# First adjacency sweep: the column sums' two halves added on VectorE, one degree matmul a tile

## What is computed

```python
A_hat = adj + jnp.eye(adj.shape[0], dtype=adj.dtype)
d_inv_sqrt = jnp.sum(A_hat, axis=1) ** (-0.5)
A_norm = d_inv_sqrt[:, None] * A_hat * d_inv_sqrt[None, :]
support = x @ W.T
out = A_norm @ support
return jax.nn.relu(out)
```

## Time and profile before

| | |
|---|---|
| median of 3 runs | 1946.84 us (1945.93 to 1947.46) |
| the profiled execution, its own time | 1950.9 us |
| its span, first to last instruction | 1949.1 us |
| mean granted TensorE clock | 0.965 |
| first sweep, in the span | to about 221 us |
| busy in the whole span | PE 1807.9, DVE 1616.5, ACT 1331.3, POOL 959.1 us |

### The profile page before, as it was taken

One profiled execution on the slowest core, in us unless ns is written; L12 is line 12 of the kernel. 1 busy time (PEld: TensorE's weight loads), 2 busy tenths in 40 slices (PEclk: granted clock), 3 DMA queues, 4 the chain that ended last, 5 costly groups with the idle time before them and its releaser, 6 DMA issues. The chain is left out here.

```text
span 1949.1 us, 41788 instructions
## 1 busy us (share of the span) xinstructions
PE 1807.9 (93%) x12680; PEld 1702.0 (87%) x12680; DVE 1616.5 (83%) x4226; ACT 1331.3 (68%) x2651; POOL 959.1 (49%) x1703
## 2 busy tenths in 40 slices
PE   6799999829999999858999979999999999999997
PEld 4689999829999999857888869999999999999997
DVE  5689878739999999738656559999999999999996
ACT  4434555416666666543555459999999999999995
POOL 2000134535555555530101027777777777777774
PEclk8889999959999999979999999999999999999999
DMA  8676778237887887543556400000000000000002
GB/s 310 207 250 201 218 200 179 96 136 215 233 234 232 236 237 228 133 170 104 193 173 203 143 17 2 2 2 2 2 1 2 2 2 2 2 2 2 2 2 71
DMA packets 97235, 226.26 MB, mean 116 GB/s; under 512 B 20897, under 2 KB 51363, under 8 KB 88620
## 3 DMA queue, kind: packets, MB, share of 16 engines
q1 hardware_dynamic: 82476, 206.33, 33.8%
q0 software_dynamic: 14592, 17.91, 4.7%
HBM read 204.43 MB, written 19.75 MB: 115 GB/s over the span
## 5 line engine op out<-in xcount | busy, mean ns | idle before, releaser
L2028 PE MATMUL ffn_psH<-ffn_w2h,ffn_vTh 128*128 128x256 f32 x1320 | 393.0, 298 | 1.5 <-DVE ffn_u L2084 1.5
L2028 PE MATMUL ffn_psH<-ffn_w2h,ffn_vTl 128*128 128x256 f32 x1320 | 374.3, 284 | 0.0
L2028 PE MATMUL ffn_psH<-ffn_w2l,ffn_vTh 128*128 128x256 f32 x1320 | 373.9, 283 | 0.0
L2117 POOL TENSOR_SCALAR ffn_vn<-ffn_vn,ffn_rstd,ffn_shift 128x256 f32<-128x256 f32 x540 | 300.0, 560 | 21.1 <-issue 1.2
L2072 DVE BATCH_NORM_STATS2 ffn_stats<-ffn_vn 128x6 f32<-128x256 f32 x780 | 284.5, 406 | 25.0 <-ACT ffn_vn L2054 23.9
L2084 DVE SCALAR_TENSOR_TENSOR ffn_u<-ffn_th,ffn_psH 128x512 f32<-128x512 f32 x390 | 263.5, 676 | 7.4 <-ACT ffn_th L2051 7.4
L2028 PEld LDWEIGHTS ffn_psH<-ffn_w2h,ffn_vTh 128*128 128x128 f32 x1320 | 253.0, 192 | 2.5 <-DVE ffn_u L2084 1.7
L2028 PEld LDWEIGHTS ffn_psH<-ffn_w2l,ffn_vTh 128*128 128x128 f32 x1320 | 253.2, 192 | 0.8
L2028 PEld LDWEIGHTS ffn_psH<-ffn_w2h,ffn_vTl 128*128 128x128 f32 x1320 | 252.5, 191 | 0.0
L2054 ACT ACTIVATE ffn_vn<-ffn_u 128x512 f32<-128x512 f32 x390 | 248.7, 638 | 0.8 <-DVE ffn_u L2084 0.8
L2051 ACT ACTIVATE ffn_th<-ffn_psH 128x512 f32<-128x512 f32 x390 | 232.6, 596 | 1.7 <-PE ffn_psH L1991 1.7
(11 more groups left out here) (240 smaller groups left out, 5021.6 us busy)
## 6 DMA issues: line engine op xcount, KB each, us to landing
g_raw<-in_adjt SPq DMA_DIRECT2D x168, 384.0 KB, 4.8
g_raw<-in_wide SPq DMA_DIRECT2D x78, 512.0 KB, 3.7
moe_w1raw<-in_wall SPq DMA_DIRECT2D x33, 1024.0 KB, 5.2
moe_w2raw<-in_wall SPq DMA_DIRECT2D x33, 1024.0 KB, 5.9
moe_b<-in_eb SPq DMA_DIRECT2D x33, 128.0 KB, 4.5
g_raw<-in_adjl SPq DMA_DIRECT2D x14, 256.0 KB, 2.8
g_raw<-in_narrow SPq DMA_DIRECT2D x13, 256.0 KB, 2.6
xn_rows<-rt_hn SPq DMA_DIRECT2D x8, 384.0 KB, 4.2
```

The costliest lines, as they stand in the source:

```text
L2028: last = pe.matmul(psH[w % R][:, q * D:(q + 1) * D], a[:, w % R, q * KD + k, :], b[:, k, :], start=(k == 0 and j == 0), stop=(k == KD - 1 ...
L2117: last = pool.tensor_scalar(vn[:, t, :], vn[:, t, :], rstd[:, s:s + 1], shift[:, s:s + 1], ALU.mult, ALU.add)
```

## The change

ScalarE's `column_sum` now copies only the second half of a panel's sums (128x384) to SBUF. A new VectorE step `fold` waits for that copy and adds the first half to it, out of PSUM, into the same buffer. TensorE's `degrees` waits for the fold and runs one matmul a tile in place of two. The steps stand later: the fold at place 2 of the next panel, TensorE's degrees at place 3 in place of 2, VectorE's at 5 in place of 4; in the second sweep the fold at turn 1, TensorE's degrees at turn 2, VectorE's at 4, the scaling at 7. Waits that protected the sums' PSUM space now wait for the fold.

```diff
--- before.py
+++ after.py
@@ -193,7 +193,7 @@
         lo = sb("g0_lo", [P, SPLITS, PANEL], F32R)
         out_t = sb("g0_out_t", [P, KD, PANEL])
         delta = sb("g0_delta", [P, PT, D])
-        colsum = sb("g0_colsum", [P, CT, PANEL])
+        colsum = sb("g0_colsum", [P, PANEL])
         rowsum = sb("g0_rowsum", [1, PANEL])
         w = sb("g0_w", [P, KD, D])
         xn = sb("g0_xn", [P, 2, D])
@@ -253,7 +253,7 @@
         rstd0_done, shift0_done, norm0_done = sem("rstd0"), sem("shift0"), sem("norm0")
         xn_done, xtr_done, xnT_done, xmm_done, sup_done = (sem(n) for n in ("xn", "xtr", "xnT", "xmm", "sup"))
         dve_added, pe_added = sem("dve_added"), sem("pe_added")
-        colsum_done, deg_mm, deg_added, deg_done = sem("colsum"), sem("deg_mm"), sem("deg_added"), sem("deg")
+        colsum_done, folded, deg_mm, deg_added, deg_done = (sem(n) for n in ("colsum", "folded", "deg_mm", "deg_added", "deg"))
         dinv_done, root_done = sem("dinv"), sem("root")
         sh_done, sl_done = sem("sh"), sem("sl")
         diag_done, hi_done, lo_done, mm_done = sem("diag"), sem("hi"), sem("lo"), sem("mm")
@@ -456,7 +456,7 @@
                 act.wait_ge(dve_added, dve_sum_of(q, dve_places(q)[-1]))
                 if q >= 1:
                     act.wait_ge(deg_mm, q)
-                last = act.activation(colsum[:, :, 0:v], deg_acc[q % 2][:, :, 0:v], ACT.Copy)
+                last = act.activation(colsum[:, 0:v], deg_acc[q % 2][:, 1, 0:v], ACT.Copy)
                 if PE_SUMS[q]:
                     act.wait_ge(pe_added, sum(PE_SUMS[:q + 1]))
                     last = act.activation(rowsum[:, 0:v], psP[0:1, 0:v], ACT.Copy)
@@ -579,11 +579,16 @@
                 dve.wait_ge(loaded[n % RING], n // RING * 16 + 16)
                 if at == 1:
                     if q >= 2:
-                        dve.wait_ge(colsum_done, q - 1)
+                        dve.wait_ge(folded, q - 1)
                     dve.tensor_tensor(to, chunk(dve_places(q)[0]), chunk(i), ALU.add).then_inc(dve_added, 1)
                 elif at > 1:
                     dve.wait_ge(dve_added, dve_sum_of(q, i) - 1)
                     dve.tensor_tensor(to, to, chunk(i), ALU.add).then_inc(dve_added, 1)
+
+            def fold(q):
+                v = width(q)
+                dve.wait_ge(colsum_done, q + 1)
+                dve.tensor_tensor(colsum[:, 0:v], deg_acc[q % 2][:, 0, 0:v], colsum[:, 0:v], ALU.add).then_inc(folded, 1)
 
             def degrees(q):
                 tiles = span_of(q)
@@ -764,7 +769,9 @@
                     for a, j in enumerate(early(q, i)):
                         split_low(early_before(q, i) + a, item(q, i), j % CT, width(q))
                     if q >= 1:
-                        if i == 4:
+                        if i == 2:
+                            fold(q - 1)
+                        if i == 5:
                             degrees(q - 1)
                         if i == 7:
                             scale_s(q - 1)
@@ -780,9 +787,11 @@
                     add_identity(m + 8)
                 if m < TURNS:
                     split_low(EARLY + m, ITEM2[m], row_tile(m) % CT, width(ORDER[PLACE[m]]))
-                if m == 3:
+                if m == 1:
+                    fold(GROUPS - 1)
+                if m == 4:
                     degrees(GROUPS - 1)
-                if m == 6:
+                if m == 7:
                     scale_s(GROUPS - 1)
                 if m == 12:
                     dve.wait_ge(root_done, 1)
@@ -902,11 +911,10 @@
                 last.then_inc(xmm_done, 1)
 
             def degrees(q):
-                pe.wait_ge(colsum_done, q + 1)
+                pe.wait_ge(folded, q + 1)
                 for i, t in enumerate(tiles_of(q)):
-                    for a in range(CT):
-                        last = pe.matmul(psD[:, t:t + 1], colsum[:, a, i * P:(i + 1) * P], g.ones[:, 0:1], start=(a == 0),
-                                         stop=(a == CT - 1 and not PE_SUMS[q]))
+                    last = pe.matmul(psD[:, t:t + 1], colsum[:, i * P:(i + 1) * P], g.ones[:, 0:1], start=True,
+                                     stop=not PE_SUMS[q])
                     if PE_SUMS[q]:
                         last = pe.matmul(psD[:, t:t + 1], rowsum[0:1, i * P:(i + 1) * P], g.ones[0:1, 0:1], start=False,
                                          stop=True)
@@ -975,7 +983,7 @@
 
             for q in range(GROUPS):
                 for i in range(CHUNKS):
-                    if i == 2 and q >= 1:
+                    if i == 3 and q >= 1:
                         degrees(q - 1)
                     if i in pe_places(q):
                         add_chunk(q, i)
@@ -993,7 +1001,7 @@
                         if 1 <= t <= NT:
                             support(t - 1)
             for m in range(END):
-                if m == 1:
+                if m == 2:
                     degrees(GROUPS - 1)
                 if m < TURNS:
                     k, j = PLACE[m], row_tile(m)
@@ -1001,7 +1009,7 @@
                         if k == 0:
                             pe.wait_ge(part_done, GROUPS - 1)
                         elif k == 1:
-                            pe.wait_ge(colsum_done, GROUPS)
+                            pe.wait_ge(folded, GROUPS)
                         else:
                             pe.wait_ge(evicted, k - 1)
                     if k == 0 and j % PT == 0:
```

## The result

| | before | changed |
|---|---|---|
| median | 1946.93 us (1943.36 to 1949.59, 10 runs) | 1942.61 us (1940.10 to 1943.76, 10 runs) |
| profiled execution, own time / span | 1950.9 / 1949.1 us | 1942.8 / 1941.0 us |

The ratio is 0.9976, with a 95% interval of 0.9969 to 0.9984: faster by 3.1 to 6.0 us. The forecast was 1943.4, or -3.4 us.

A forecast was written before the change was run, and what follows sets the result against it. No single engine bounds the sweep; TensorE or VectorE leads panel by panel. Terms -1.2 - 0.8 + 0 + 0.5 - 1.4 - 0.5 = -3.4 us take the 1946.84 median to 1943.4 us, range 1940.8 to 1947.4.

The forecast's parts named there:

- the rival that had the clock give more: Panel 3's half-clock stretch ends, say, 3.4 us sooner, freeing 1.7 us of work: -5.1 us, 1941.7; chance 0.15.
- Panel 1: First sweep, panel 1: six fewer TensorE passes save 0.70 us, the wait for ScalarE's copy is covered: -0.7 us.
- Panel 2: Panel 2 to panel 3's start: the late loads move by the same -0.7 us, hiding anything else panel 2 gains or loses.
- Panels 3 and 4: Sum reaches -1.2 us after panel 3, TensorE the bound; panel 4's degrees end 0.8 us sooner, making -2.0.
- I take -1.2, near the second: Panel 3: -2.1 us if the half-clock stretch moves with the work, -1.05 if it ends near 102; -1.2 taken.
- Panel 5: Panel 5: the degree wait of 0.43 us is about the fold's price and VectorE does not idle behind it: 0.
- Panel 6: Panel 6: VectorE is full with no degree wait to give back, TensorE's six passes become idle time: +0.5 us.
- Panels 7, 8 and the last degrees: Panels 7 and 8: TensorE leads, twice -0.7 us; second sweep's last degrees: four passes fewer, -0.5 us.
- The moved places: Degrees one place later: same price in panel 1, about 1 us later for VectorE in panel 3 but slack; no term.
- VectorE becomes the bound in panels 7 and 8: Those panels each cost a fold instead of saving 0.7 us, last degrees give nothing: about -0.5 us, 1946.3; chance 0.23.
- VectorE ends every panel: From panel 3 on, degrees behind twelve matmuls, no wait given back, every fold paid: slower, 1950.9 us; chance 0.10.
- signs of being wrong: Panel 4's degree wait unshortened; TensorE idle for low parts in panels 3, 7 or 8; half-clock stretches other than 88 to 102.

The follow-up runs named there:

- places_kept: Changed kernel with TensorE's and VectorE's degrees back at their old places and the fold at place 1: 1940.36 us, ratio 0.9963 against the kernel before.
- fold_one: Kernel before with half copy, fold and single matmul a tile only for panel 2's sums: 1945.0 us, ratio 0.9988.
- moves_only: Kernel before with the degrees one place later as in the change, but no fold: 1947.42 us, ratio 1.0007.
- passes4: Changed kernel with three more matmuls a tile against a zero column, 208 passes for 52: 1961.74 us, ratio 1.0077 against the kernel before.
- fold2: Changed kernel with one more unread 128x384 VectorE add ahead of each fold: 1944.44 us, ratio 0.9991 against the kernel before.
- experiment 9: Changed kernel with the slot table's 73-row filling issued as two transfers, 64 and 9 rows: 1939.3 us, ratio 0.9961 against the kernel before.

## Why the prediction was right, and where it was not

The sum forecast -3.4 us; the medians show -4.3, the stages -5.1. The measured time lies in the forecast's own range, 1942.0 to 1944.3, but that is in part luck: panels 3 and 4 gave 2.1 us more than their terms, panels 5 to 8 with the last degrees 0.6 less, and -5.1 is the sum of the rival that had the clock give more.

**Panel 1: right.** Forecast -0.7, measured -0.74 (16.78 to 16.04). The changed kernel's TensorE timeline shows the step with the degrees, against the earlier trace rows:

```profile
50.94 1.10 PE L910 MATMUL g_psR<-g_w,g_xnT 128*128 128x256 f32 x4 [0.35 <-ACT l_s L452]
51.87 0.72 PE L916 MATMUL g_psT<-ones,g_colsum 128*128 128x1 f32 x6
52.71 1.03 PE L910 MATMUL g_psR<-g_w,g_xnT 128*128 128x256 f32 x4
```

It lasts 52.71 - 50.94 = 1.77 us; 1.75 was forecast. The new wait of 8.66 us for ScalarE's copy cost nothing that shows in this stage, as argued. The Trainium skill, page "TensorE: Matmul & The Clock Gate", section "Back-to-back issue gap", gives its 81 ns for a matmul of 128 columns, while the passes here have one. The 0.74 us for six passes, 0.12 each, decides for the row.

**Panel 2: right.** To panel 3's first add it gives 0.2 beyond panel 1's 0.7: the landing moved along with the train ahead of it.

**Panels 3 and 4: the failed step.** Beyond their starts, the forecast had about -0.5 for panel 3 and -0.8 for panel 4; measured are -1.3 and -2.0. The step was "I take -1.2, near the second, because the stretch begins at 88, before TensorE's first matmul of the panel". It asked only where the half-clock stretch stands, at fixed length, and put a shorter one among the rivals, with a stretch ending 3.4 us sooner. It was 10 us shorter (13.7 to 3.4). With it the bound changed: the forecast had TensorE without a gap in panel 3, and VectorE's lateness as slack. In the changed kernel VectorE waits for nothing behind the panel's first add, and TensorE stands for its low part:

```profile
98.34 0.45 PE L939 MATMUL g_acc<-g_hi,g_sh 128*128 128x384 f32 x1 [1.52 <-DVE g_lo L616]
```

Shown is that the stretch at panel 3's start is short in every execution with the folds everywhere, and long in every one of before. It is also shown that its length doesn't depend on the degrees' place alone: places_kept has it short with before's place. Nor does the number of narrow passes in panel 3 order it. That is 18 in before (12 of line 908, 6 of line 911) and 12 in the changed kernel, but fold_one has 12 too and kept 10.2 us, moves_only has 18 and showed 6.8 and 3.4, and passes4 has 30 and showed 3.4 twice. One rival fits all eleven profiles with the late load and was not tested: the moment at which the clock falls. In the three of before it fell 0.6 to 1.2 us ahead of TensorE's first matmul of the panel, in moves_only 1.2 and in fold_one 0.6; there the stretch lasted 6.8 us or longer. In places_kept, fold2 and passes4 it fell 0.2 to 0.35 ahead, in the three of the changed kernel with that matmul or up to 0.45 behind it; there it lasted 3.4. Whether the change sets this moment, and whether the moment sets the length, stays open. What the 10 us are worth can't be separated cleanly either. The two panels gave 3.4 us where the forecast, at before's clock, had 1.3; the 2.1 left over are what the clock and the shifted order account for together.

**Panel 5: near, by luck.** Forecast 0, measured -0.3. Two of the three executions of before have two half-clock stretches of 3.4 us in or next to this panel; the third has none and took 22.88. Against that one, with the clock alike, the changed kernel's 23.2 is 0.3 *longer*.

**Panel 6: the number right.** Forecast +0.5, measured +0.7. TensorE was busy 20.53 of 22.00 us and now

```profile
145.90:168.50 22.60, 19.77 (x113) 18.81 (x112) 22.08 (x41) 10.69 (x22) 0.85 (x1) 1.00 0.73 229
```

so its idle time went from 1.5 to 2.8, the forecast's "some 1 us"; VectorE stays full. But the +0.5 holds for the place at which the change puts the fold, not for the fold as such: places_kept takes 21.93 us here, before 21.89. In both kernels the first low part starts 2.2 us after the panel's first add (2.15 in before), and with the old places the fold stands ahead of it, in time that VectorE loses there anyway (VectorE's timeline of places_kept):

```profile
143.90 0.96 DVE L583 TENSOR_TENSOR g_psT<-g_raw 128x768 f32<-128x768 f32 x1
144.77 0.55 DVE L591 TENSOR_TENSOR g_colsum<-g_acc,g_colsum 128x384 f32<-128x384 f32 x1
...
146.10 1.02 DVE L616 TENSOR_TENSOR g_lo<-g_raw,g_hi 128x384 fp32r<-128x384 f32 x2
```

In the changed kernel, whose panel 6 starts at 145.94, it stands behind the low parts and costs 149.53 - 149.06 = 0.47 us:

```profile
148.11 1.03 DVE L616 TENSOR_TENSOR g_lo<-g_raw,g_hi 128x384 fp32r<-128x384 f32 x2
149.06 0.55 DVE L591 TENSOR_TENSOR g_colsum<-g_acc,g_colsum 128x384 f32<-128x384 f32 x1
149.53 0.96 DVE L586 TENSOR_TENSOR g_psT<-g_psT,g_raw 128x768 f32<-128x768 f32 x1
```

**Panels 7, 8 and the last degrees: too much.** Forecast were -0.7, -0.7 and -0.5, that is -1.9; measured is -1.25. The step that failed is that moving the places is free ("TensorE leads; VectorE's wait of 1.43 pays for its fold"). With the old places it does come to -1.8 (57.29 against 59.05), and moved places without the fold lose 0.7. So the terms fit the fold, and the move takes a part back.

**The moved places** were costed at nothing, and take 2.9 us by the table of places_kept. TensorE stands for low parts within panels 5 and 6 of the changed kernel:

```profile
138.67 0.45 PE L939 MATMUL g_acc<-g_hi,g_sh 128*128 128x384 f32 x1 [2.25 <-DVE g_lo L616]
...
160.77 0.44 PE L939 MATMUL g_acc<-g_hi,g_sh 128*128 128x384 f32 x1 [1.69 <-DVE g_lo L616]
```

places_kept has shorter ones at both places:

```profile
136.62 0.44 PE L939 MATMUL g_acc<-g_hi,g_sh 128*128 128x384 f32 x1 [1.38 <-DVE g_lo L616]
...
158.08 0.44 PE L939 MATMUL g_acc<-g_hi,g_sh 128*128 128x384 f32 x1 [1.07 <-DVE g_lo L616]
```

In panel 6 it is mostly the fold's place (above). In the other panels, which of the moved pieces does it (the fold, TensorE's degrees or VectorE's) was not tried apart.

**The rivals.** "The clock gives more" came in part, as a larger term inside the forecast's course, and was given back in the moved places. "VectorE becomes the bound in panels 7 and 8" did not come: no wait stands before the degrees at 177.06, and the stage shrank. "VectorE ends every panel" did not come either; but its mechanism, degrees behind twelve matmuls and low parts late, is what panels 3, 5 and 6 show in small, and all that is left of the change once the late load is gone (experiment 9). The degree wait in panel 4 fell from 2.81 to 1.01 us, just over the limit of 1 us that I had set. Two of the signs of being wrong did show: TensorE stood 1.52 us for a low part in panel 3, and the half-clock stretch was another than at 88 to 102.

## What to carry to other kernels

When two engines share the lead, price an edit per stage, and price the reordering that comes with it as an edit of its own: here, by the stage lengths, the kernel with the fold at the old places was about 8 us shorter in the sweep, some of it by the clock, and the new places that came with the change cost 2.9. A stretch at half clock in the profile of before is not fixed: state it as a range of lengths, and profile both kernels several times before crediting an edit with it. And ask first why an engine stands idle ahead of the stage: one split transfer gave more by the median than the whole change (8 us against 4), and beside it the change as made showed no gain.

## What the runs showed of the hardware

- **One transfer of 73 rows held up the loads behind it.** The loads next in the queue after the 73-row filling landed in 13.0 to 13.9 us; after fillings of 64 and 9 rows, in 4.1 to 5.4. This was worth 0.41% of the kernel. The Trainium skill, page "DMA: Bandwidth & Descriptors", section "Why a DMA increments its semaphore by 16 and not by 1", says that a transfer is spread over the largest number of engines, up to 16, that divides the slowest dimension of both its sides, here the rows. By that 73 rows, a prime number, use one engine, 64 use sixteen and 9 use nine. The landing times agree; no run here shows the engines or tries another row count.
- **Half-clock stretches** differ in place and number between executions of one kernel (two after panel 3 in two executions of before, none in the third), but the one at panel 3's start, behind the same wait for a load, repeated its length three times of three in both kernels (13.7 and 3.4 us).
- **A 128x1 pass on full weights cost 0.12 us** with its weight load: 0.74 us for the six that panel 1 lost. The 156 that experiment 6 added come to the same on average, with more half clock among it.
